# Transfers of the softmax shift rows issued by the sync engine's queue in place of ScalarE's

## The reference

```python
x = x + xattn(layernorm(x), ctx, ctx, lens, Wq, Wk, Wv, Wo)      # cross attention, 77 keys, the first lens[b] count
x = x + ffn(layernorm(x), ...)
# ffn: a mixture attention
pooled = h.mean(1); logits = relu(pooled @ gw1.T + gb1) @ gw2.T + gb2
top_vals, top_idx = top_k(logits, 2); gates = softmax(top_vals)
# each of q, k, v, o: x @ Wm.T + sum over the 2 experts of ((x @ V[e].T) * S[e]) @ U[e].T * gate[e] + b
q = moe(h, q...) * 32 ** -0.5; k = moe(h, k...); v = moe(h, v...)
attn = softmax(q @ k.T)                                          # per head, 512 x 512
out = moe(attn @ v, o...)
```

## Time and profile before

| what | value |
|---|---|
| runs | 1422.53, 1422.72, 1434.18 us; median 1422.72 |
| profiled execution, span from first to last instruction | 1426.7 us (its own time is not listed apart) |
| PE busy | 1391.0 us, 97% |
| DVE busy | 951.9 us, 67% |
| ACT busy | 861.3 us, 60% |
| POOL busy | 679.8 us, 48% |
| SP's transfers (queue q1) | 74,007 packets, 128.55 MB |
| ACT's transfers (queue q10) | 4,672 packets, 1.17 MB |
| chain that ended last | PE 85%, ACT 7%, issue 2%, DMA 2%, POOL 2%, DVE 1% |

### The profile page before, as it was taken

The page is one execution under the profiler, slowest core; times in us unless marked ns, Lnnn a source line. Parts: engine busy times, 40 slices in busy tenths (PEclk is TensorE's granted clock), DMA queues, the critical chain, the costliest instruction groups (busy, mean ns, idle before and its releaser), DMA issues.

```text
span 1426.7 us, 17122 instructions
## 1 busy us (share of the span) xinstructions
PE 1391.0 (97%) x5704; PEld 702.4 (49%) x5704; DVE 951.9 (67%) x1687; ACT 861.3 (60%) x1499; POOL 679.8 (48%) x411
## 2 busy tenths in 40 slices
PE   8998999999999999999999999999999999999987
PEld 5545444545455444555555445455545454444432
DVE  4454577766767677767777677767777677666572
ACT  2425474866577663975658664876648665565652
POOL 2011143545555362556445463555625455465675
PEclk9889999999999999999999999999999999999999
DMA  7514233522434224522234224332235323233210
GB/s 252 143 53 133 46 68 96 153 76 46 98 110 108 75 54 125 137 61 76 68 111 123 75 59 135 110 85 67 58 104 152 76 46 97 64 101 79 81 39 30
DMA packets 78767, 130.81 MB, mean 92 GB/s; under 512 B 26374, under 2 KB 32134, under 8 KB 75607
## 3 DMA queue, kind: packets, MB, share of 16 engines
q1 hardware_dynamic: 74007, 128.55, 33.4%
q10 hardware_dynamic: 4672, 1.17, 0.4%
HBM read 66.08 MB, written 12.21 MB: 55 GB/s over the span
## 4 chain that ended last, share of the span: by engine, by line
PE 85%; ACT 7%; issue 2%; DMA 2%; POOL 2%; DVE 1%; ACTq 0%; SPq 0%; POOLq 0%
PE pj L1217 43%; PE scT L1302 9%; PE sc L1274 8%; PE acc L1331 7%; PE sc L1263 4%; PE pj L1247 2%; PE pj L1311 2%; PE scT L1295 2%; PE pj L1319 2%; PE pj L1340 2%; DMA qs<-shift 2%; PE pj L1190 1%; ACT xhat L810 1%; PE pj L1202 1%; PE pj L1211 1%
## 5 line engine op out<-in xcount | busy, mean ns | idle before, releaser
L925 ACT ACTIVATE probs<-scT 128x512 f32<-128x512 f32 x512 | 288.9, 594 | 303.9 <-PE scT L1302 300.8
L1048 DVE TENSOR_REDUCE negmax<-sc 128x1 f32<-128x512 f32 x512 | 338.0, 684 | 140.7 <-PE sc L1274 139.7
L784 POOL TENSOR_TENSOR probs_sum<-probs_sum,probs 128x1024 f32<-128x1024 f32 x128 | 300.2, 2365 | 57.4 <-ACT probs L925 57.3
L1075 DVE RECIPROCAL inv_sum<-pj 128x128 f32<-128x128 f32 x256 | 225.0, 921 | 59.9 <-PE pj L1340 39.2
L1274 PE MATMUL sc<-ks,qs 96*128 96x512 f32 x512 | 260.1, 541 | 2.4 <-DVE negmax L1048 1.6
L1217 PE MATMUL pj<-XT,Wqk 128*128 128x512 f32 x512 | 257.3, 598 | 0.6 <-DVE Wqk L1140 0.6
L1302 PE MATMUL scT<-qs,ks 99*128 99x512 f32 x512 | 250.9, 517 | 6.2 <-DMA qs<-shift 3.2
L780 POOL TENSOR_TENSOR probs_sum<-probs 128x1024 f32<-128x1024 f32 x64 | 151.4, 2372 | 173.8 <-ACT probs L925 173.8
L790 POOL TENSOR_TENSOR uv_stack<-UVS_sb,uv_stack 96x1024 fp32r<-96x1024 f32 x32 | 75.7, 2367 | 178.1 <-ACT UVS_sb L832 178.1
L1302 PEld LDWEIGHTS scT<-qs,ks 99*128 99x128 f32 x512 | 94.7, 191 | 124.5 <-ACT probs L925 60.4
L754 POOL TENSOR_TENSOR xhat<-xhat,inv_sum 128x128 f32<-128x128 f32 (+1 forms) x56 | 45.1, 806 | 207.7 <-DVE inv_sum L1075 207.7
(11 more groups left out here) (103 smaller groups left out, 1716.6 us busy)
## 6 DMA issues: line engine op xcount, KB each, us to landing
Wqk<-in_WmT SPq DMA_DIRECT2D x16, 1024.0 KB, 6.1
Wvo<-in_WmT SPq DMA_DIRECT2D x16, 1024.0 KB, 6.5
UVS_sb<-in_UVS SPq DMA_DIRECT2D x64, 192.8 KB, 3.4
qs<-stage_lo SPq DMA_DIRECT2D x136, 64.0 KB, 2.2
qs<-qs SPq DMA_DIRECT2D x34, 256.0 KB, 3.0
X<-in_x SPq DMA_DIRECT2D x8, 1024.0 KB, 6.0
ks<-stage_lo SPq DMA_DIRECT2D x128, 64.0 KB, 2.0
ks<-ks SPq DMA_DIRECT2D x32, 256.0 KB, 3.0
```

The costliest lines, as they stand in the source:

```text
L784: nc.gpsimd.tensor_tensor(probs_sum[:, pair], probs_sum[:, pair], probs[:, kt % 2, pair], ALU.add)\
L925: nc.scalar.activation(probs[:, kt % 2, jj, :], scT[:, ST[step], :], ACT.Exp, scale=SCALE)\
L1048: nc.vector.tensor_reduce(negmax[:, 0, n:n + 1], sc[:, SC[step], :], AX.X, ALU.max, negate=True)\
L1075: nc.vector.reciprocal(inv_sum[:, INV[use], at], pj[:, PJ[left_in(full)], at])\
```

## The change

The two steps `shift_move` and `cross_shift_move`, with the helper `move_shift`, go from ACT's program to SP's. Their places in the list stay; the waits on `shift_hi` and `shift_lo` and the 128 issues are made by SP now, between its other transfers. Buffers, semaphores and all other steps stay as they are.

```diff
@@ @block.sync
+            def move_shift(side, dst, done, b, turn):
+                for part, split in enumerate(("shift_hi", "shift_lo")):
+                    sp.wait_ge(split, sp.after(split, *turn))
+                    row = SHIFT_ROW + part
+                    queue.dma_start(dst[row:row + 1].rearrange("p j (t n) -> p (j t) n", n=P).bitcast(F32),
+                                    shift[side * SIDE:side * SIDE + HJ * TT, part, :].bitcast(F32)).then_inc(sems[done], 16)
+
+            def shift_move(step, b, j):
+                move_shift(0, qs[:, slot_of(j)], "shift_moved", b, ("shift", b, j))
+
+            def cross_shift_move(step, b, i):
+                move_shift(1, cross_stack(b, i), "cross_shift_moved", b, ("cross_shift", b, i))
...
-                     "residual2": residual2})
+                     "residual2": residual2, "shift_move": shift_move,
+                     "cross_shift_move": cross_shift_move})
@@ @block.scalar
-            def move_shift(side, dst, done, b, turn):
...
-            def shift_move(step, b, j):
...
-            def cross_shift_move(step, b, i):
...
-                      "q1_rows": q1_rows, "qk_rows": qk_rows, "shift_move": shift_move, "cross_shift_move": cross_shift_move, "csT": csT, "sT": sT,
+                      "q1_rows": q1_rows, "qk_rows": qk_rows, "csT": csT, "sT": sT,
```

More of the change, by code:

```diff
@@ L894, in qk_rows @@
                                          ACT.Copy).then_inc(sems["rows_copied"], 1)
-            def move_shift(side, dst, done, b, turn):
[L897 to L901, removed]
-            def shift_move(step, b, j):
-                move_shift(0, qs[:, slot_of(j)], "shift_moved", b, ("shift", b, j))
-            def cross_shift_move(step, b, i):
-                move_shift(1, cross_stack(b, i), "cross_shift_moved", b, ("cross_shift", b, i))
             def csT(step, b, i, j):
```

## The result

The changed kernel takes 1473.07 us (median of four runs, 1464.95 to 1473.47) against 1422.62 us for the kernel before in the same session: a ratio of 1.0329, 95% interval 1.0285 to 1.0374. It is 3.3% slower; 1464 us was predicted, and 1473 lies in the range.

The account below looks back on a forecast made before the run. The prediction took the kernel's middle to be bound by PE, busy 163.02 of 163.90 us per period. Terms 20.4 + 5.4 + 2 + 13.6 = 41.4 us, added to the 1422.7 us median, gave 1464 us; range 1440 to 1478.

Parts of the forecast that it names:

- The seven places: Job 2's shift_move ahead of job 3's stacks, batches 0 to 6: PE waits, usually losing 2.8 us, 20.4 in all.
- the one at the start: Batch 1's cross_shift_move, job 0, ahead of batch 0's value-weight load: PE loses 5.4 us, bounds 0.9 and 6.6.
- ACT's relief at zero: Taking the 64 steps' issues off ACT gains nothing; bounds zero and a 12.7 us gain.
- The wait: PE ahead of the job-3 scores idles 3.0 us at a usual place, of which 2.8 us is lost.
- The clock: PE's clock halves for 3.41 us after each of 8 waits: 1.7 us each, 13.6 us; bounds 0 and 27.
- the second rival: The waits come and the low clock lasts twice as long after each: 55 us, so 1478 us; chance 0.12.
- The first rival: The waits come but PE's clock stays up: 27.8 us, so 1450 us; chance 0.22.
- The rule that stood beside it: Only idle gaps longer than expected here lower PE's clock; without falls the sum is 28 instead of 42 us.
- The other places: The other 56 places: three late by under a microsecond each; 2 us in all, bounds 0 and 4.
- the further falls: Extra low-clock time after each wait, beyond the forecast; half of it was said to set the range's top, 1478 us.
- only the start would cost: Rival: the job-3 stacks land early enough, leaving 9 us of loss, so 1432 us; chance 0.05.
- PE would find the stacks in place: Rival: job-3 stacks are in when PE comes and ACT's relief remains: at most 12.7 us gained, 1410 us; chance 0.06.

Follow-up runs that it names:

- e1: The changed kernel with the shift_move steps of job 2 in batches 0 to 6 given back to ACT: 1435.71 us, 1.0082.
- e2: The kernel before with only the shift_move steps of job 2 in batches 0 to 6 moved to SP: 1460.62 us, 1.0271.
- e7: The kernel before with only the cross_shift_move step of batch 1, job 0, moved to SP: 1434.08 us, 1.0058.
- e5: e3 with the cross_shift_move step of batch 1, job 0, also put behind the load of the value weights: 1423.36 us, 1.0006.
- e3: The changed kernel with the job-2 shift step of batches 0 to 6 issued behind both job-3 stacks, all on SP: 1433.78 us, 1.0074.
- e8: Against the kernel before, SP issues only 24 shift steps with nothing urgent behind them, ACT the other 40: 1420.05 us, 0.9979.
- e11: e10 with four needless matmuls ahead of PE's wait for the job-3 stacks, as in e6: 1454.36 us, 1.0192.
- e10: The changed kernel with the key-weight load of batches 1 to 6 behind the next batch's first qsc stack: 1468.54 us, 1.0327.
- e4: The changed kernel with the job-2 shift step of batches 0 to 6 between the two job-3 stacks: 1449.69 us, 1.0156.
- e6: The changed kernel with four needless matmuls ahead of PE's wait for the job-3 stacks in batches 0 to 6: 1478.72 us, 1.0376.
- e12: e4 with the 1 MB key-weight load of batches 1 to 6 issued by ACT's queue instead of SP's: 1435.81 us, 1.0088.

## Why the prediction was right, and where its terms were off

**The mechanism.** The seven places and the one at the start are the right ones: e1, e2 and e7 find the loss there and e5 takes it all away by moving those steps. The signs named in advance came: the first issue of the stacks is 7.4 us later against the cast than before (from 6.0 us ahead of its end to 1.3 behind it), PE's wait ahead of the job-3 scores is released by `ks`, the clock falls behind it.

**ACT's relief at zero.** Nearly right. With the loss taken away `sT` no longer waits for its shift rows, and a regular period is 0.5 us shorter (e3, e5, e8), some 3 us over the kernel; e8 shows 0.2% of it, and in e5 other waits use it up. In the changed kernel it is part of the net loss below.

**The wait: mis-sized.** The step "2.8 us" for a usual place was too small. PE's wait was put at 3.0 us and is 3.6. SP's last copy is issued 6.97 us after the cast's end (617.05 less 610.08), not 6.8, and lands 3.2 us later, not 3.0; and PE is there 6.66 us after the cast (620.35 - 3.61 - 610.08) instead of 6.98. The last 0.3 us, `sT`'s 0.22 us of idle time and a little more, lengthen the wait and lose nothing, since PE only stands idle later. The net loss is then some 3.3 us where 2.8 was counted. The same half microsecond is missing elsewhere: against the cast the scores of job 3 come 3.6, 3.2, 3.3, 3.2, 3.2, 2.6 and 4.6 us later than before, batches 0 to 6 in order, 23.6 in all where 20.4 was counted. Batch 5 is the least and batch 6 the most, as forecast (2.1 and 4.3). That the period of batch 6 grew by only 3.5 us has to do with the clock, which was low there in the kernel before too. For the other six batches I had 16.1 us of waits and 10.2 of clock, 26.3 in all; their periods grew by 31.4, of which 19.0 are the waits by this count.

**The clock: nearly right in mean, wrong in form.** 1.7 us per place was the term; e11 against e10 gives 2.0 at six places. In the trace it comes as 3.4 us of low clock at four of the seven places (batches 0, 1, 2 and 4) and 6.8 at three, so the second rival, twice as long each time, held in part. Of the 6.8 us PE still waits through 0.8, 1.5 and 3.1 us, which cost nothing more. The first rival, waits without a fall, is out: the clock fell at all seven. The rule that stood beside it, of the Trainium skill, "TensorE: Matmul & The Clock Gate", section "HAM oscillation — how this bites in real kernels", is not refuted by these falls alone, since the wait came out longer than forecast; but the falls after five of the six waits of 1.45 to 2.19 us in e4 disagree with it, as the earlier trace rows did, while the waits of 1.97 and 2.25 us in e6, without a fall, do not. By that rule the clock would have fallen at the start all the same, where the wait was put at 5.4 us, so the 28 us that stand beside it are about 2 too few. The price, about 2 us a place, is the measured one whichever holds.

**The start: mis-sized by the same term.** The wait was put at 5.4 us and is 5.72; the clock was low for 6.83 us and not 3.41. PE works through 5.00 of these, so 2.5 us are lost to it where 1.7 were counted. Sum 8.2, against 7.1 predicted and 8.9 in the spans, of which 0.2 us belongs to the next term; what the other 0.5 is, is not shown. The other places, put at 2 us, are three waits for `ks` that the kernel before does not have, 0.22 us in batch 0 and 1.12 and 0.94 in batch 7: 2.3.

**Sum and range.** The like of the 41.4 us forecast is the growth of the traced span, 45.0; the rest of the way to 50.5 lies in which executions were traced. The upper bound of 1478 was said to hold half of the further falls, but it holds all of them: half would be 1471, under the 1473 measured. That 1473 lies in the range owes something to this slip.

**The other rivals.** That only the start would cost (1432 us) is out by e1 and e2; that PE would find the stacks in place and ACT's relief would win is out by the seven waits of the change itself.

**What the working did not see.** "Where the steps behind the job-3 stacks come later too, their use comes later with PE" held in the changed kernel only because PE was held up as well. Moved from 5.2 to 0.5 us behind a 1 MB load, the `qsc` stack's copy lands after 9.0 us instead of 3.2. This second deadline is why e4 and e6 missed their forecasts; the chain that ended last runs, in two neighbouring batches of the changed kernel, once through the one stack and once through the other:

```profile
279.42 3.27 DMA ks<-ks
...
454.35 8.09 DMA qsc<-qsc
```

Left open: what decides between 3.4 and 6.8 us of low clock after waits of equal length, and whether a wait of about 2 us is followed by one at all.

## What to carry to other kernels

On an engine that issues transfers in program order, a wait costs what stands behind it: list the next issues, when each is used, and by whom, before a step with a wait is moved there. Where such a wait stands can matter more than whose queue it stands in (1.0329 against 1.0006 here, by order alone). And when a late transfer is repaired, look for the next one on the same queue before the gain is counted: its landing time is not a constant but depends on what was issued just ahead of it.

## What the runs showed of the hardware that I had not expected

- A copy of 256 KB takes 2.9 us from issue to landing (median), 7.5 to 9.0 us when its stack is issued 0.5 us behind a load of 1 MB on the same queue, and 5.2 to 7.6 with that load on another queue (e12). The load is stretched too, from 6.3 to 7.9 us in the kernel before to 9.9 to 11.4 in the changed one; on the other queue it takes 5.8 to 7.6.
- Waits of 1.45 to 2.19 us in e4 were followed by a low clock in five of six cases, and of the two waits of 1.45 us one was (in batch 3) and one not (in batch 0). In e6 waits of 1.97 and 2.25 us were not, one of 2.18 us was. So in these traces the length of a wait near 2 us does not settle it. After the 3.16 us of e6 the low clock lasted 13.6 us, four times as long as the shortest seen.
